# A routed mixture-of-experts stage on one core: every expert's gate and up weights are split once and kept, the chosen slab comes by a DMA inside SBUF, and the loops are written out

## What is computed

```python
x = x + L0(x)      # per-sequence matrix: cond-weighted sum of 8 masked matrices, plus bias
x = x + L1(x)      # shared matrix plus cond-weighted LoRA
x = x + L2(x)      # MoE: per sequence the top-2 experts of 8, plus one shared expert
x = x + L3(x)      # per sequence the argmax expert: silu(up) * gate, down, with biases

# L2, one expert (128 -> 512 -> 128):
g = x @ gate_w; u = x @ up_w
out = (gelu(g) * u) @ down_w          # times the expert's routing weight
# L3, one expert (128 -> 256 -> 128):
hidden = silu(x @ Wu.T + bu) * (x @ Wg.T + bg)
out = hidden @ Wd.T + bd
```

## Time and profile before

| | |
|---|---|
| time, median of 3 runs (lowest to highest) | 156.12 us (155.41 to 158.0) |
| span of the profiled execution | 152.1 us |
| PE busy, share of the span | 139.3 us, 92% |
| DVE | 137.1 us, 90% |
| ACT | 114.0 us, 75% |
| POOL | 95.7 us, 63% |
| granted PE clock | full in every slice |
| DMA | 13.42 MB, nearly all before 35 us and after 140 us |

### The profile page before, as it was taken

One profiled execution on the slowest core, in us unless ns is written; L12 is line 12 of the kernel. 1 busy time (PEld: TensorE's weight loads), 2 busy tenths in 40 slices (PEclk: granted clock), 3 DMA queues, 4 the chain that ended last, 5 costly groups with the idle time before them and its releaser, 6 DMA issues.

```text
span 152.1 us, 4268 instructions
## 1 busy us (share of the span) xinstructions
PE 139.3 (92%) x928; PEld 125.3 (82%) x928; DVE 137.1 (90%) x239; ACT 114.0 (75%) x221; POOL 95.7 (63%) x106
## 2 busy tenths in 40 slices
PE   6799969999999999999989899898998999998882
PEld 5468838888888979999989899798997989887861
DVE  0796998786779799999999999999999999999993
ACT  3406759545567978999989899798997889978670
POOL 0204807500005759787998979789797887899560
PEclk9999999999999999999999999999999999999999
DMA  2999999980000000000000000000000000000124
GB/s 49 327 378 425 423 420 415 420 359 15 0 2 0 0 0 6 0 4 0 0 0 0 0 0 0 0 0 0 0 0 0 0 0 0 0 4 0 37 79 164
DMA packets 4330, 13.42 MB, mean 88 GB/s; under 512 B 736, under 2 KB 2016, under 8 KB 4192
## 3 DMA queue, kind: packets, MB, share of 16 engines
q1 hardware_dynamic: 4320, 13.31, 22.7%
HBM read 12.26 MB, written 1.05 MB: 88 GB/s over the span
## 4 chain that ended last, share of the span: by engine, by line
PE 62%; DVE 18%; issue 7%; DVEq 3%; ACT 2%; DMA 2%; POOL 2%; POOLq 1%; ACTq 1%; SPq 0%
PE gate L264 24%; PE up L264 19%; PE acc L264 17%; DVE h_lo L823 3%; DMA const_sb<-consts 2%; DVEq L219 2%; DVE h_full L839 2%; DVE w_hi L914 1%; POOL w_lo L655 1%; DVE h_full L837 1%; PE spare L264 1%; DVE rest L727 1%; DVE x_in L928 1%; ACT L589 1%; DVE h_lo L975 1%
## 5 line engine op out<-in xcount | busy, mean ns | idle before, releaser
L663 POOL TENSOR_TENSOR w_lo<-w_all,w_hi 128x256 fp32r<-128x256 f32 (+1 forms) x40 | 36.2, 904 | 28.8 <-ACT w_hi L536 26.8
L823 DVE TENSOR_TENSOR h_lo<-h_full,h_hi 128x512 fp32r<-128x512 f32 x55 | 46.6, 848 | 0.0
L655 POOL TENSOR_TENSOR w_lo<-w_all,w_hi 128x256 fp32r<-128x256 f32 x40 | 42.7, 1068 | 1.0 <-DVE w_hi L914 0.6
L527 ACT ACTIVATE h_hi<-h_full 128x512 fp32r<-128x512 f32 x55 | 34.5, 627 | 7.9 <-DVE h_full L839 4.3
L521 ACT ACTIVATE h_act<-gate 128x512 f32<-128x512 f32 x48 | 28.2, 588 | 10.3 <-PE gate L264 9.7
L264 PE MATMUL gate<-x_hi,w_hi 128*128 (+1 forms) x80 | 24.5, 307 | 4.9 <-DVE h_full L839 2.6
L861 DVE TENSOR_TENSOR w_lo<-w_all,w_hi 128x256 fp32r<-128x256 f32 (+1 forms) x40 | 26.9, 673 | 0.8 <-ACT w_hi L536 0.8
L536 ACT ACTIVATE w_hi<-w_all 128x512 fp32r x40 | 25.3, 632 | 1.6
L839 DVE SCALAR_TENSOR_TENSOR h_full<-h_act,w_route,up 128x512 f32<-128x512 f32 x32 | 23.5, 735 | 0.0
L264 PE MATMUL gate<-x_hi,w_lo 128*128 (+1 forms) x80 | 22.5, 282 | 0.0
L264 PE MATMUL gate<-x_lo,w_hi 128*128 (+1 forms) x80 | 22.5, 282 | 0.0
(11 more groups left out here) (133 smaller groups left out, 290.2 us busy)
## 6 DMA issues: line engine op xcount, KB each, us to landing
w_all<-slabs SPq DMA_DIRECT2D x12, 768.0 KB, 15.8
x_in<-xT SPq DMA_DIRECT2D x1, 1024.0 KB, 6.2
outT<-x_in SPq DMA_DIRECT2D x8, 128.0 KB, 1.9
w_all<-slabs SPq DMA_DIRECT2D x2, 384.0 KB, 7.0
w_l_sb<-w_l SPq DMA_DIRECT2D x2, 256.0 KB, 3.7
lin_sb<-lin SPq DMA_DIRECT2D x1, 256.0 KB, 3.7
const_sb<-consts SPq DMA_DIRECT2D x1, 80.0 KB, 3.1
bias_row<-l_bias SPq DMA_DIRECT2D x1, 64.0 KB, 3.6
```

The source lines that it names most:

```text
L527: nc.scalar.activation(h_hi[:, slot, :], h_full[:, slot, :], ACT.Copy).then_inc(h_hi_done, 1)
L655: nc.gpsimd.tensor_tensor(w_lo[:, slot, SLAB_GU:], w_all[:, bass.ds(at + SLAB_GU, SLAB - SLAB_GU)], w_hi[:, slot, SLAB_GU:].bitcast(F32), ...
L663: nc.gpsimd.tensor_tensor(w_lo[:, slot, split:SLAB_GU], w_all[:, bass.ds(at + split, n)], w_hi[:, slot, split:SLAB_GU].bitcast(F32), ALU.s ...
L823: V.tensor_tensor(h_lo[:, slot, :], h_full[:, slot, :], h_hi[:, slot, :].bitcast(F32), ALU.subtract).then_inc(h_lo_done, 1)
```

## The change

**Layout.** `slabs` holds 24 slabs of `WIDE` = 1280 columns: 512 for the rounded gate and up, 512 where the raw gate and up land and where `lo` is then written over them, 256 for raw down. The shared slabs have their own `sh_raw`. To make room, x is loaded into `x_res` and worked on there, `h_full` has three slots instead of four, and the buffers of the first layers (`w_l0_sb`, `m_b` and others, through `early`) lie in the place of the L3 slabs 3 to 7; so the last three L3 loads wait for the end of `x2` (`x2_sum`).

**Splitting once.** During the shared units ACT rounds gate and up of each whole expert (2 slabs, 1024 columns) at the units of `HI_UNIT`; POOL subtracts six experts (`LO_POOL`, 1024 columns each), DVE the four slabs of the other two (`LO_DVE_UNIT`, 512 columns each). The eight L3 slabs are rounded by ACT (`HI_L3_Q`) and subtracted by POOL (`LO_L3_Q`, two at a time) during the routed units 2 to 17. The per-unit splitting of gate and up on ACT, DVE and POOL is gone. Down is still split in each unit, now ACT and POOL alone, and in the unit of q itself.

**The slab to its slot.** SP waits until all experts are split, and then for each of the 40 slabs loads the address and issues a DMA of 128 x 1024 float32 (hi and lo of gate and up, 512 KB) from `slabs` to one of four slots `w_gu`, from the fifth on once the gate and up matmuls of the slot's last user are done. PE waits for that DMA.

**Loops.** All `Fori` loops are written out. POOL's bias products and DVE's sum over them move from the shared part into the routed part.

```diff
+WIDE = 2 * SLAB_GU + 256
-GU_DVE = 256
-GU_DVE_L3 = 128
-DVE_ROUNDS = 2
+HI_UNIT = {1: 0, 2: 1, 4: 2, 5: 3, 7: 4, 8: 5, 10: 6, 11: 7}
+LO_POOL = (0, 1, 2, 3, 4, 6)
+LO_DVE_UNIT = {10: 10, 11: 11, 13: 14, 14: 15}
+HI_L3_Q = {2 * e + 2: e for e in range(E)}
+LO_L3_Q = {4 * k + 5: k for k in range(E // 2)}
...
             for e in range(E):
-                at = slice(e * HALVES * SLAB, (e + 1) * HALVES * SLAB)
-                sp.dma_start(w_all[:, at], slabs[:, at]).then_inc(d_experts, DMA)
...
+                sp.dma_start(slabs[:, 2 * e:2 * e + 2, RAW_AT:], slabs_moe[:, 2 * e:2 * e + 2, :]).then_inc(d_expert[e], DMA)
+            for k in range(E // 2):
+                if k == 1:
+                    sp.wait_ge(x2_sum, PAIRS)
+                first = SLABS_EXPERTS + 2 * k
+                sp.dma_start(slabs[:, first:first + 2, RAW_AT:], slabs_l3[:, 2 * k:2 * k + 2, :]).then_inc(d_l3[k], DMA)
+
+            sp.wait_ge(table_ready, 1)
+            sp.wait_ge(moe_lo_pool, len(LO_POOL))
+            sp.wait_ge(moe_lo_dve, len(LO_DVE_UNIT))
+            for q in range(PREPS):
+                if q == UNITS_ROUTED:
+                    sp.wait_ge(l3_lo, E // 2)
+                if q >= W_SLOTS:
+                    sp.wait_ge(up_ready, R0 + q - W_SLOTS + 1)
+                at = slab_of(sp, q)
+                sp.dma_start(w_gu[:, q % W_SLOTS, :].bitcast(F32),
+                             slab_cols(at, 0, 2 * SLAB_GU)).then_inc(d_gu[q % W_SLOTS], DMA)
...
+            def weights_here(q):
+
+                pe.wait_ge(d_gu[q % W_SLOTS], (q // W_SLOTS + 1) * DMA)
...
                 banks_free(u, False)
-                pe.wait_ge(gu_hi_done, q + 1)
-                pe.wait_ge(gu_lo_done, q + 1)
-                pe.wait_ge(gu_lo2_done, q + 1)
...
+                weights_here(q)
...
+            def round_expert(e):
+
+                act.wait_ge(d_expert[e], DMA)
+                nc.scalar.activation(hi_part(2 * e, 2).bitcast(F32R), raw_part(2 * e, 2), ACT.Copy).then_inc(moe_hi, 1)
...
+            gelu(0)
+            for u in range(1, UNITS_SHARED):
+                gelu(u)
+                round_h(u - 1)
+                if u < 4 and u + 1 < PAIRS:
+                    x2(u + 1)
+                if u in HI_UNIT:
+                    round_expert(HI_UNIT[u])
...
+            for e in LO_POOL:
+                pool.wait_ge(moe_hi, e + 1)
+                nc.gpsimd.tensor_tensor(raw_part(2 * e, 2).bitcast(F32R), raw_part(2 * e, 2), hi_part(2 * e, 2),
+                                        ALU.subtract).then_inc(moe_lo_pool, 1)
...
+            def lo_half(s):
+
+                dve.wait_ge(moe_hi, s // 2 + 1)
+                V.tensor_tensor(raw_part(s, 1).bitcast(F32R), raw_part(s, 1), hi_part(s, 1),
+                                ALU.subtract).then_inc(moe_lo_dve, 1)
...
+            for u in range(1, UNITS_SHARED):
+                product(u)
+                lo_h(u - 1)
+                if u == UNITS_SHARED - 4:
+                    normalise()
+                if u >= 4 and u % 4 == ACC_AT:
+                    add_acc(u // 4 - 1, PAIR, u - ACC_AT)
+                if u in LO_DVE_UNIT:
+                    lo_half(LO_DVE_UNIT[u])
```

## The result

The changed kernel takes 159.69 us in the median of 5 runs (158.74 to 161.76), against 156.12 before (155.41 to 158.0): ratio 1.024, 95% interval 1.017 to 1.031. It is slower by about 2.4%. The forecast was 157.8 us, its range 151.5 to 162.5.

The account below looks back on a forecast made before the run. Shared part bound by PE, routed part and L3 by DVE. Span 152.1 + 1.3 + 4.3 + 0.6 + 4.6 - 6.6 + 1.0 - 3.5 = 153.8, plus 4.0 gives 157.8 us; range 151.5 to 162.5.

Parts of the forecast that it names:

- What bounds the kernel: Shared part bound by PE, routed part and L3 by DVE; without splitting PE sets the pace there, -6.6 and -3.5 us.
- +1.0 collisions: Routed units: POOL's instructions, L3 subtractions among them, hold up DVE and cost 1.0 us of the gain.
- ACT's two roundings ahead of a gelu: Start of the shared part: two roundings delay the gelu of unit 3 and so unit 5, +1.3 us.
- The lock: Shared part: two-SBUF-operand DVE and POOL instructions exclude each other for their whole length; five units cost 0.86 each, +4.3 us.
- Expert 6 and DVE's halves: Shared part from unit 10: POOL's sixth subtraction and DVE's four halves hold one product back, +0.6 us.
- The first slab: Ahead of unit 16: PE waits for DVE's last half, SP's address and the copy of slab 0, +4.6 us.
- The clock: Units 16 and 17: PE's clock falling in the wait for slab 0; not in the sum, only a rival of +2 us.
- PE comes back slow: Rival: after the wait for slab 0 units 16 and maybe 17 run at the lower clock, +2 us, 159.9; chance 0.17.
- The loops: Whole kernel: written-out loops save jumps but bring more code to fetch; put at 0, bounds 0 to 2 us.
- From span to time: End of the sum: 4.0 us added because the median of the runs, 156.12, lies that far above the profile's span.
- splitting is nearly free: Rival: shared-part collisions of 4.9 us shrink to 0 to 2, later 1.0 goes too; 151.9 to 154.9 us; chance 0.28.

Follow-up runs that it names:

- e4_act_later: Changed kernel with ACT's roundings of the experts in units 3 to 12 instead of 1 to 11: 158.56 us, ratio 1.018 to the kernel before.
- e3_no_pool_lo: Changed kernel with POOL's six expert subtractions narrowed to 4 columns, leaving those low parts wrong: 154.08 us, ratio 0.991 to the kernel before.
- e2_pool512: Changed kernel with POOL's six subtractions of 1024 columns made as twelve of 512: 157.12 us, ratio 1.003 to the kernel before.
- e1_warm: Changed kernel with 22 stand-in matmuls on PE between unit 15 and the wait for slab 0: 157.42 us, ratio 1.012 to the kernel before.
- e6_before_unrolled: Kernel before the change with its seven hardware loops written out, nothing else touched: 156.55 us, ratio 1.005 to the kernel before.
- e5_halves_earlier: Changed kernel with DVE's last two halves in units 12 and 13 instead of 13 and 14: 156.68 us, ratio 1.008 to the kernel before.
- e9_dve_splits: Changed kernel with 12 low halves on DVE, POOL only experts 0 and 1 in 512-column pieces, ACT rounding in units 3 to 10: 153.87 us, ratio 0.982.
- e11_again: Changed kernel measured and profiled once more, nothing altered: 159.68 us, ratio 1.023 to the kernel before.
- e8_start: Changed kernel with five warm-up products instead of four and one more ahead of the wait for lora_bw: 157.86 us, ratio 1.013.

## Why the prediction came out as it did

The time lay inside the range, 1.9 us above the forecast. Nearly all of that is one term that the sum did not have, the clock; the errors of the others, between -0.6 and +0.8 us, happen to cancel, which is luck. By the forecast's own steps:

- *What bounds the kernel:* right. With the splitting out of the routed part PE is full and its pace is 2.16 us (forecast 2.15). The units from 16 on give back 9.7 us at full clock (93.93 - 39 x 2.16); 10.1 were forecast before collisions, 9.1 with them. The term "+1.0 collisions" in the routed part was wrong: there PE never waits (68.90 of 68.90 us), since DVE has the slack to sit out POOL's L3 subtractions.
- *ACT's two roundings ahead of a gelu:* 1.44 against 1.3; e4_act_later removes exactly that.
- *The lock:* units 5 to 10 are 2.81 us apart on the mean (forecast 2.9), 3.87 in all against 4.3. e3_no_pool_lo and e2_pool512 show the mechanism, not only the size. The Trainium skill, page "SBUF — State Buffer", section "SBUF: two separate sides", says it as a rule: a GpSimd instruction and a VectorE one with two SBUF inputs exclude each other for a whole instruction. The rows here agree.
- *Expert 6 and DVE's halves:* 0.75 against 0.6; without POOL's subtractions (e3_no_pool_lo) it is 0.
- *The first slab:* 5.37 against 4.6. Each link of the chain was put a little short: the last half 1.3 us behind the moment at which unit 16 was due (56.58 + 2.04; forecast 0.9), SP 1.0 (0.7), the copy 3.1 (2.9). The bounds by loads and stores held. (The forecast's own times give a wait of 60.1 - 55.6 = 4.5; it summed 4.6.)
- *The clock:* this is the step that failed. "PE comes back slow" was named as a rival, with 0.17 and +2 us, and it was what happened: +2.2 us in the first profile, 1.5 in the second. The forecast took every step of the chain as likely and then gave the clock a sixth, because no row of before showed a fall. No row of before showed an idle PE of that length either; the absence was no evidence. The page "TensorE: Matmul & The Clock Gate" of the Trainium skill, section "HAM oscillation — how this bites in real kernels", says that a wait for a DMA between matmuls can throttle the array again. The trace agrees (PE idle 5.19 us, clock 0.50 behind it), and e1_warm, where PE doesn't idle and keeps 1.00, bears it out.
- *The loops:* put at 0; e6_before_unrolled measured 0.8 us (0.1 to 1.5) for the kernel before. In the changed kernel no stretch shows it: with POOL's subtractions left out, units 5 to 15 take 20.49 us against 20.40 before.
- *From span to time:* 4.0 us were added as the distance of the median from the span. About 1.8 of it lie around every span (161.76 to 160.0); the rest is that the profile of before was short for its kernel: the 56 executions of the same kernel that were taken beside the experiments have spans from 152.3 to 156.0, in the median 154.2. A part of this is likely the start, since no profile here has an earlier unit 0 than that of before (14.87) and most have it 0.5 to 2 us later. The changed kernel begins like that too, so the 4.0 us held for it: 156.12 plus the change's own +3.2 to +3.9 us is 159.3 to 160.0, and 159.69 was measured.

Some small slips in the forecast move nothing else: 157.8 and 2 more are 159.8, not 159.9; and the upper end of "splitting is nearly free", with 2 us of collision and the later 1.0 gone, is 153.9, not 154.9.

What would have told beforehand: the price of the wait was computed to a microsecond, and a term of 4.6 us of idle PE deserved the clock term beside it in the sum, not in a rival. And the trace of before did hold matmuls at the lower pace, under a clock column of 1.00: its two `w0` products of eight matmuls take 1.50 us at 5.26 and 1.05 at 8.91.

## What to carry to other kernels

When work is moved from a stage with one bound into a stage with slack, count not only the slack but the longest single instruction that a neighbour has to sit out, and cut it: the same columns in twelve pieces instead of six were worth 2%. When all later work is made to wait for the last piece of a batch, the cost is the chain behind that piece (last piece, issue, landing), and then what the idle engine needs to come back to speed. Filling the wait with idle work took the second part away (e1_warm); an earlier last piece shortened the first, and in the one profile of e5_halves_earlier the second went with it. Take the distance between a profile's span and the median apart before adding it: part of it can be that the profile caught a short execution.

## What the runs showed of the hardware

- TensorE kept its clock in the profile of e5_halves_earlier, where it had idled 2.83 us, and fell to 0.50 where it idled longer at this place (3.45 us in e9_dve_splits, 5.19 in after, 5.20 in e11_again). The two units at the lower level cost 1.5 to 2.6 us. The length of the one idle time is not all that counts: at the start of e11_again it fell within an idle time of 1.40 us.
- At the start of the kernel eight matmuls of the same shape take 1.92 or 1.05 us depending on the run, with the granted clock shown as 1.00 in both (after, e8_start); where the array had risen before and fell back, the column shows it (0.50 in e11_again, 1.71 us). Unit 0 begins between 14.87 and 18.05 us in kernels with the same start, about 2% of the time, more than most edits here.
- DVE's `h_lo`, with two operands in SBUF, takes 2.15 to 2.29 us instead of 0.68 beside POOL's subtractions of 1024 columns, and 1.2 us at most in the same units beside those of 512; the product, with one operand in PSUM, keeps its 0.68.
- A copy of 512 KB inside SBUF lands in the median 2.9 to 3.1 us after its issue, at up to 418 GB/s, no slower than a load; in each kernel the slowest of the 40 took 4.8 to 5.3 us.
